# Expert outputs of a decoder layer: from one DRAM row per pick to two running sums per token

## The chip, the cores and the metric

The kernel runs on one core of a Trainium2 chip. The metric is device microseconds of one execution; lower is better. Times below are the median of several runs, and the profile is of one further execution.

## What is computed

One decoder layer over 8 sequences of 128 tokens with 256 features, so 1,024 tokens. Self-attention (sliding window) and cross-attention come first and are each added to the residual; the change touches only the feed-forward part that follows. That part is, cut to what matters:

```python
shared = silu_and_mul(x @ shared_gate_up_w.T) @ shared_down_w.T      # 704 hidden units
shared = shared * sigmoid(x @ sgate_w.T)
topk_w, topk_ids = top_k(softmax(x @ gate_w.T), 4)                   # 16 experts, 4 picks per token
for e in range(16):
    coef = sum(where(topk_ids == e, topk_w, 0), axis=-1)
    acc = acc + (silu_and_mul(x @ w13[e].T) @ w2[e].T) * coef[:, None]
out = x_residual + shared + acc
```

So every token receives the sum of four expert outputs, each 256 float32 numbers (1 KB).

## The kernel before

The program is written by hand for each engine: SP issues plain DMAs in the order written, GpSimd (POOL) issues indirect DMAs, and semaphores tie the engines together. A tile is the 128 tokens of one sequence; there are B = 8 tiles.

**Routing and blocks.** Once a tile's top four experts are known, GpSimd scatters each token row into `x_slots` in DRAM, sorted by expert (line 534, 32 indirect DMAs). The sorted rows are then worked off in NBLK = 47 blocks of 128 rows, each block of one expert; rows in a block that hold no token are padding.

**The block stage.** For block n, SP loads 128 token rows (`xb`, `load_rows`, line 426) and the expert's down weights (`w2`, `load_down`, line 433), in turn, one of each per block. TensorE (PE) turns the rows, computes gate and up, turns the hidden rows and computes the down product. VectorE (DVE) scales the result by the routing weight into one of RB = 4 buffers `yb` (`take_block`, line 1271). It also works out `ids`, the 128 DRAM rows to which the block's output goes (`block_ids`, line 1280). GpSimd's `place_rows` (line 607) then scatters the 128 rows of `yb` to `y_picks` in DRAM: one row per pick, 4,096 in all, and rows of their own behind them for padding. No row is written twice, and `place_rows` waits for nothing but its `yb` and its `ids`. `take_block` n waits until the scatter of block n - 4, which read the same buffer, has landed (`yb_placed`).

**The end.** TensorE still has the second half (tiles 4 to 7) of the shared expert to do: chunks 6 to 11, as `down(6)`, `rows_of(8)`, `down(7)`, `rows_of(9)`, and so on to `down(11)`. `rows_of(n)` computes gate and up products of chunk n, `down(n)` its down product; each `down(n)` needs `hid_h` and `hid_l` of its chunk, which ScalarE (ACT) and DVE make. Beside that, SP waits for the landing of all 47 scatters and loads `y_picks` back into `yg`, one DMA of 512 KB for each tile (line 451), four rows per token. DVE adds the four rows of a token and the residual in `combine`, three instructions per tile. These stand in DVE's queue between the chunk work in a fixed order: `gated(8)`, `low_hidden(8)`, two tiles of `combine`, `gated(9)`, `low_hidden(9)`, two tiles, `gated(10)`, `low_hidden(10)`, two tiles, `gated(11)`, `low_hidden(11)`, one tile, `finish(1)`, one tile, then the four additions of the shared result (line 1329). `gated` (line 1160) is the first DVE step of a chunk and `low_hidden` (line 1165) the last; between them ACT makes `hid_h` (line 743). `finish` (line 1171) copies half of the down result out, `turn_rows` (line 1651) turns it. Tiles 0 to 3 are stored after their `combine`, tiles 4 to 7 after the additions of line 1329.

`link(ins)` makes DVE wait for the instruction's own completion before its next one.

**Zeros.** While attention runs, SP also fills `x_slots` with zeros from the tile `zero_b` (line 412, 16 DMAs). `load_keys(7)` is the last DMA of that loop; after it SP waits for the shared weights and loads two small tables (lines 417, 418).

Of the kernel before, what the change touches and what calls it, by code (L numbers as in the profile page):

```python
# [7 lines left out]
F32 = mybir.dt.float32  # L8
# [5 lines left out]
ALU = mybir.AluOpType  # L14
# [3 lines left out]
B, T, D = 8, 128, 256  # L18
# [9 lines left out]
TOPK = 4  # L28
# [11 lines left out]
RB = 4  # L40
# [4 lines left out]
YROW = PICKS + NBLK * 128  # L45
# [13 lines left out]
def decoder_layer(nc, x_in, ctx_in, keys_in, wqkv_in, bqkv_in, wo_in, bo_in, rope_in, masks_in, gate_in,  # L59
                  w13_in, w2_in, shared_in, ident_in, iota_in, tri_in, upto_in, table_in, picks_in, dump_in, packs_in, out):  # L60
    ctx = ExitStack()
    with ctx:
# [6 lines left out]
        def sem(name):  # L69
            return ctx.enter_context(nc.semaphore(name))  # L70
# [5 lines left out]
        def place(name, shape, dt=F32):  # L76

            n = 1
            for extent in shape[1:]:
                n *= extent  # L80
            at = cursor[0]
            cursor[0] = at + -(-n * mybir.dt.size(dt) // 32) * 32
            return nc.alloc_sbuf_tensor_at(name, shape, dt, offset=at)
# [91 lines left out]
        yg = place("yg", [128, B, TOPK, D])  # L175
# [53 lines left out]
        y_picks = nc.dram_tensor("y_picks", [YROW, D], F32)  # L229
# [136 lines left out]
        gathered = [sem(f"gathered{b}") for b in range(B)]  # L366
# [12 lines left out]
        def _(sp):  # L379
# [35 lines left out]

            sp.wait_ge(swl_ready, SC)
# [33 lines left out]
            for b in range(B):  # L450
                sp.dma_start(yg[:, b, :, :], y_picks[T * TOPK * b:T * TOPK * (b + 1), :].rearrange("(p k) d -> p k d", k=TOPK)
                             ).then_inc(gathered[b], 16)

            for b in range(B):
                sp.wait_ge(x_out_ready, b + 1)
                sp.dma_start(out[b], x2[:, b, :]).then_inc(y_stored, 16)
            sp.wait_ge(y_stored, 16 * B)
# [3 lines left out]
        def _(pool):  # L461
# [141 lines left out]
            def place_rows(n):  # L603

                pool.wait_ge(yb_ready, n + 1)
                pool.wait_ge(ids_ready, n + 1)
                pool.indirect_dma_start(y_picks[:, :], bass.IndirectOffsetOnAxis(ids[:, n:n + 1], 0),  # L607
                                        yb[:, n % RB, :], None).then_inc(yb_placed[n % RB], 16)
# [230 lines left out]
        def _(dve):  # L839
# [5 lines left out]
            def link(ins):  # L845

                links[0] += 1
                ins.then_inc(chain1, 1)
                dve.wait_ge(chain1, links[0])
# [449 lines left out]
            def combine(first, last):  # L1299

                for b, step in (divmod(i, 3) for i in range(first, last)):
                    if step == 0:
                        dve.wait_ge(gathered[b], 16)
                        link(dve.tensor_tensor(yg[:, b, 0:2, :], yg[:, b, 0:2, :], yg[:, b, 2:4, :], ALU.add))  # L1304
                    elif step == 1:
                        link(dve.tensor_tensor(yg[:, b, 0, :], yg[:, b, 0, :], yg[:, b, 1, :], ALU.add))
                    else:
                        ins = dve.tensor_tensor(x2[:, b, :], yg[:, b, 0, :], x2[:, b, :], ALU.add)
                        if b < HB:
                            ins.then_inc(x_out_ready, 1)  # L1310
                        else:
                            link(ins)

            dve.wait_ge(rows_added, HB)
            done = 0
            for n, more in zip(range(SC + AHEAD, 2 * SC), (6, 6, 6, 0)):
                gated(n)
                low_hidden(n)
                combine(done, done + more)
                done += more  # L1320
            combine(done, done + 3)
            finish(1)
            combine(done + 3, 3 * B)
# [480 lines left out]
def lay_out(inputs):  # L1804
# [51 lines left out]
    pick = np.arange(PICKS, dtype=f).reshape(B, T, TOPK) - f(UNPLACED)  # L1856
    got["picks_in"] = pick.transpose(1, 0, 2)
    got["dump_in"] = (PICKS + np.arange(128)[:, None] + 128 * np.arange(NBLK)[None, :]).astype(f)
# [18 lines left out]
```

## Time and profile before

| what | value |
|---|---|
| median of 3 runs | 355.84 us |
| lowest and highest run | 354.18 and 358.53 us |
| profiled execution, its own time | 359.31 us |
| span of the profiled execution | 357.5 us |
| PE busy | 312.9 us (88% of the span) |
| DVE busy | 247.5 us (69%) |
| ACT busy | 186.6 us (52%) |
| POOL busy | 149.0 us (42%) |
| mean granted TensorE clock | 0.944 of full speed |

The span runs from the first to the last recorded work of the core, and 1.81 us of the execution's own time lie outside it. Attention and routing fill the first 206 us of the span. The block stage runs to about 327 us; the first scatter of block outputs starts at 218.2 us. The end takes the remaining 30 us. A row of the timeline gives the start and the duration in us, the engine, the line and the operation, and in brackets how long the engine sat idle before it and who released it. A count such as x2 or x8 means that many instructions merged in one row.

### The profile page before, as it was taken

The page shows a single profiled execution, that of the slowest core. Times are in us where ns is not written, and L with a number is a line of the kernel's source. Part 1 is how long each engine was busy: PE and PEld are TensorE (multiplying, and loading weights), DVE is VectorE, ACT ScalarE, POOL GpSimd, SP SyncE. Part 2 cuts the span into 40 slices and gives each one's busy share as a digit, 9 for nine tenths or more (in the row PEclk, how much of TensorE's full clock was granted, in tenths as well). Part 3 has the DMA queues.
Part 4 walks back from the last instruction along what each step waited for, and adds up shares of the span by engine and source line. Part 5 has one row for each costly group of instructions (what it writes and reads, how often), then busy time and mean ns, then how long its engine had stood idle before and what let it go on. Part 6 is the DMA issues. An engine that isn't in the chain of part 4 may idle for free.

```text
span 357.5 us, 8484 instructions
## 1 busy us (share of the span) xinstructions
PE 312.9 (88%) x2594; PEld 242.3 (68%) x2595; DVE 247.5 (69%) x733; ACT 186.6 (52%) x537; POOL 149.0 (42%) x179
## 2 busy tenths in 40 slices
PE   8857799999999997869989569998999999899953
PEld 3334576767667775647767459887888989798732
DVE  2353778888888769574878966666667767673785
ACT  1033689898898858467368314343444444332210
POOL 2580424435554304177876832344343444434000
PEclk9986999999999879996999959999999999999996
DMA  5996086989799831012232524777677777773931
GB/s 206 287 397 265 4 243 201 300 226 312 236 254 282 234 102 31 0 63 108 78 110 77 149 64 149 228 221 223 202 227 221 220 226 231 217 210 103 380 132 59
DMA packets 44185, 66.84 MB, mean 187 GB/s; under 512 B 5379, under 2 KB 32020, under 8 KB 43636
## 3 DMA queue, kind: packets, MB, share of 16 engines
q1 hardware_dynamic: 39508, 54.91, 51.0%
q0 software_dynamic: 3792, 10.56, 7.9%
q10 hardware_dynamic: 848, 0.92, 0.8%
q8 instruction: 19, 0.31, 0.4%
q14 instruction: 18, 0.15, 0.1%
HBM read 37.07 MB, written 29.30 MB: 186 GB/s over the span
## 4 chain that ended last, share of the span: by engine, by line
PE 35%; issue 23%; POOL 16%; DVE 13%; ACT 6%; DMA 4%; SPq 0%; POOLq 0%; DVEq 0%; ACTq 0%
POOL y_picks L607 12%; PE bank L1492 7%; PE bank L1418 6%; PE bank L1409 5%; PE bank L1362 4%; POOL x_slots L534 3%; PE bank L1427 3%; ACT probs L644 2%; PE bank L1451 2%; PE bank L1404 2%; PE bank L1530 2%; PE bank L1466 2%; DVE yg L1304 1%; DVE neg_max L895 1%; DMA yg<-y_picks 1%
## 5 line engine op out<-in xcount | busy, mean ns | idle before, releaser
L607 POOL DMA_INDIRECT y_picks<-yb,ids x47 | 45.1, 959 | 73.9 <-DVE yb L1271 73.3
L644 ACT ACTIVATE probs<-bank,neg_max 128x128 f32<-128x128 f32 x256 | 70.6, 401 | 2.8 <-DVE neg_max L895 2.8
L895 DVE TENSOR_REDUCE neg_max<-bank 128x4 f32<-128x512 f32 x64 | 42.1, 683 | 11.8 <-PE bank L1409 11.6
L1762 PE MATMUL bank<-w,hbt 128*128 128x256 f32 x188 | 48.2, 380 | 0.0
L1418 PE MATMUL bank<-ident,probs 128*128 128x128 f32 x256 | 39.8, 297 | 3.0 <-ACT probs L644 3.0
L534 POOL DMA_INDIRECT x_slots<-x,slots x32 | 36.7, 1147 | 10.8 <-issue 8.9
L1418 PEld LDWEIGHTS bank<-ident,probs 128*128 128x128 f32 x256 | 31.6, 152 | 11.6 <-ACT probs L644 7.8
L804 ACT ACTIVATE xbt_h<-bank 128x256 fp32r<-128x256 f32 x47 | 18.1, 384 | 40.1 <-PE bank L1732 40.0
L1762 PEld LDWEIGHTS bank<-w,hbt 128*128 128x128 f32 x188 | 32.1, 190 | 2.5
L1264 DVE TENSOR_TENSOR hb<-sg,bank 128x176 f32<-128x176 f32 x47 | 15.8, 337 | 24.4 <-ACT sg L812 24.4
L812 ACT ACTIVATE sg<-bank 128x176 f32<-128x176 f32 x47 | 14.9, 317 | 30.4 <-PE bank L1492 30.4
L1732 PE MATMUL bank<-ident,xb 128*128 128x128 f32 x94 | 19.1, 287 | 10.4 <-POOL w_l L600 7.4
L1492 PE MATMUL bank<-w_h,xbt_h 128*128 x94 | 27.6, 375 | 0.0
L1256 DVE TENSOR_TENSOR xbt_l<-bank,xbt_h 128x256 fp32r<-128x256 f32 x47 | 19.9, 424 | 9.7 <-ACT xbt_h L804 5.8
L1271 DVE TENSOR_SCALAR yb<-bank,offset 128x256 f32<-128x256 f32 x47 | 22.7, 483 | 2.6 <-PE bank L1762 2.6
L1732 PEld LDWEIGHTS bank<-ident,xb 128*128 128x128 f32 x94 | 12.8, 146 | 17.2 <-issue 7.6
L1492 PE MATMUL bank<-w_h,xbt_l 128*128 x94 | 23.4, 331 | 0.0
L1492 PE MATMUL bank<-w_l,xbt_h 128*128 x94 | 23.3, 330 | 0.0
L481 POOL TENSOR_TENSOR turned<-qkv,rope 128x320 f32<-128x320 f32 x8 | 6.9, 865 | 37.2 <-DVE qkv L876 37.2
L743 ACT ACTIVATE hid_h<-hid 128x512 fp32r<-128x512 f32 x12 | 7.6, 632 | 28.3 <-DVE hid L1160 28.3
L505 POOL TENSOR_TENSOR rstd<-ve,expo 128x1 f32<-128x1 f32 x16 | 9.4, 590 | 28.5 <-DVE ve L945 28.4
L1752 PE MATMUL bank<-ident,hb 128*128 128x128 f32 x94 | 18.2, 275 | 1.3 <-issue 1.2
(175 smaller groups left out, 694.9 us busy)
## 6 DMA issues: line engine op xcount, KB each, us to landing
x_slots<-zero_b SPq DMA_DIRECT2D x16, 1072.0 KB, 10.5
w<-w_in_dram SPq DMA_DIRECT2D x47, 256.0 KB, 3.1
xb<-x_slots SPq DMA_DIRECT2D x47, 134.0 KB, 2.8
w<-w_in_dram SPq DMA_DIRECT2D x4, 1408.0 KB, 12.9
yg<-y_picks SPq DMA_DIRECT2D x8, 512.0 KB, 7.1
sw_raw<-shared_in_dram SPq DMA_DIRECT2D x6, 384.0 KB, 3.3
ktc<-keys_in_dram SPq DMA_DIRECT2D x8, 256.0 KB, 3.0
ctx_sb<-ctx_in_dram SPq DMA_DIRECT2D x1, 1024.0 KB, 13.3
```

The source lines that it names most:

```text
L534: pool.indirect_dma_start(x_slots[:, :], bass.IndirectOffsetOnAxis(slots[:, TOPK * b + k:TOPK * b + k + 1], 0), x[:, b, :], None).then_inc ...
L607: pool.indirect_dma_start(y_picks[:, :], bass.IndirectOffsetOnAxis(ids[:, n:n + 1], 0), yb[:, n % RB, :], None).then_inc(yb_placed[n % RB] ...
L644: ins = act.activation(probs[:, g, j, :], ps_s[kind][g][:, 128 * j:128 * j + 128], ACT.Exp, bias=neg_max[:, kind, g, j:j + 1])
L804: act.activation(xbt_h[:, n % 2, :, :], ps_xt[n % 2][:, 0:KC * 128].rearrange("p (k n) -> p k n", k=KC), ACT.Copy).then_inc(xbt_high, 1)
L895: dve.tensor_reduce(neg_max[:, kind, g, :], ps_s[kind][g].rearrange("p (j n) -> p j n", j=BLK), AX.X, ALU.max, negate=True).then_inc(max_r ...
L1256: dve.tensor_tensor(xbt_l[:, n % 2, :, :], ps_xt[n % 2][:, 0:KC * 128].rearrange("p (k n) -> p k n", k=KC), xbt_h[:, n % 2, :, :].bitcast( ...
L1271: dve.tensor_scalar(yb[:, n % RB, :], ps_yb[n % 2][:, 0:D], offset[:, n % RB, 1:2], None, ALU.mult).then_inc(yb_ready, 1)
L1418: ins = pe.transpose(ps_s[kind][g][:, 128 * j:128 * j + 128], probs[:, g, j, :], ident[:, :])
L1492: ins = pe.matmul(outs, w, m, start=first and i == 0, stop=last and i == len(todo) - 1, skip_group_check=not (first and last))
L1732: ins = pe.transpose(ps_xt[n % 2][:, 128 * k:128 * k + 128], xb[:, n % RB, 128 * k:128 * k + 128], ident[:, :])
L1752: ins = pe.transpose(ps_ht[n % 2][:, 128 * k:128 * k + 128], hb[:, n % 2, 128 * k:128 * k + 128], ident[:, :])
L1762: ins = pe.matmul(ps_yb[n % 2][:, 0:D], hbt[:, n % 2, k, :], w2[:, n % RB, k, :], start=k == 0, stop=k == KC - 1)
```

## The change

Block outputs are no longer placed in a row of their own. GpSimd's scatter becomes an adding one: each block's 128 rows are added to rows of one of two arrays in DRAM, `y_sum0` and `y_sum1`, which have one row per token. Even blocks go to the first, odd blocks to the second. A token's four experts fall into different blocks, and two additions to one row may not overlap, so scatter n now waits until scatter n - 2 has landed. The two arrays are filled with zeros by two DMAs of 1 MB during attention, and the first two scatters wait for them. At the end two rows per token are loaded, in four DMAs (two halves by two sums) of 512 KB each, and `combine` handles two tiles in two instructions: sum plus sum, then plus residual. `combine(3)`, the last, now stands ahead of `finish(1)`. Tiles 0 to 3 are stored in two DMAs in place of four. The tables of row numbers hold the token's row in place of the pick's. The diff, without the declarations of semaphores and without the index tables:

```diff
-YROW = PICKS + NBLK * 128
+YROW = B * T + NBLK * 128
+SUMS = 2
...
-        yg = place("yg", [128, B, TOPK, D])
+        yg = place("yg", [128, SUMS, B, D])
...
-        y_picks = nc.dram_tensor("y_picks", [YROW, D], F32)
+        y_sums = [nc.dram_tensor(f"y_sum{i}", [YROW, D], F32) for i in range(SUMS)]
...
+            for i in range(SUMS):
+                sp.dma_start(y_sums[i][0:B * T, :].rearrange("(p r) d -> p r d", p=128),
+                             zero_b[:, 0:2 * D].bitcast(F32).unsqueeze(1).broadcast_to([128, B, D])).then_inc(sums_zeroed, 16)
+
             sp.wait_ge(swl_ready, SC)
             sp.dma_start(ends[:, :, :, :], table_in).then_inc(table_loaded, 16)
...
             for r in range(RB):
                 sp.wait_ge(yb_placed[r], 16 * len(range(r, NBLK, RB)))
-            for b in range(B):
-                sp.dma_start(yg[:, b, :, :], y_picks[T * TOPK * b:T * TOPK * (b + 1), :].rearrange("(p k) d -> p k d", k=TOPK)
-                             ).then_inc(gathered[b], 16)
-
-            for b in range(B):
-                sp.wait_ge(x_out_ready, b + 1)
+            for half in range(NHALF):
+                for i in range(SUMS):
+                    sp.dma_start(yg[:, i, HB * half:HB * half + HB, :],
+                                 y_sums[i][0:B * T, :].rearrange("(p b) d -> p b d", b=B)[:, HB * half:HB * half + HB, :]
+                                 ).then_inc(gathered[half], 16)
+
+            for pair in range(HB // 2):
+                sp.wait_ge(x_out_ready, pair + 1)
+                sp.dma_start(out[2 * pair:2 * pair + 2].rearrange("b p d -> p b d"), x2[:, 2 * pair:2 * pair + 2, :]
+                             ).then_inc(y_stored, 16)
+            for b in range(HB, B):
+                sp.wait_ge(x_out_ready, HB // 2 + b - HB + 1)
                 sp.dma_start(out[b], x2[:, b, :]).then_inc(y_stored, 16)
...
                 pool.wait_ge(yb_ready, n + 1)
                 pool.wait_ge(ids_ready, n + 1)
-                pool.indirect_dma_start(y_picks[:, :], bass.IndirectOffsetOnAxis(ids[:, n:n + 1], 0),
-                                        yb[:, n % RB, :], None).then_inc(yb_placed[n % RB], 16)
+                if n < SUMS:
+                    pool.wait_ge(sums_zeroed, 16 * SUMS)
+                else:
+
+                    pool.wait_ge(yb_placed[(n - SUMS) % RB], 16 * ((n - SUMS) // RB + 1))
+                pool.indirect_dma_start(y_sums[n % SUMS][:, :], bass.IndirectOffsetOnAxis(ids[:, n:n + 1], 0),
+                                        yb[:, n % RB, :], None, compute_op=ALU.add).then_inc(yb_placed[n % RB], 16)
...
-            def combine(first, last):
-
-                for b, step in (divmod(i, 3) for i in range(first, last)):
-                    if step == 0:
-                        dve.wait_ge(gathered[b], 16)
-                        link(dve.tensor_tensor(yg[:, b, 0:2, :], yg[:, b, 0:2, :], yg[:, b, 2:4, :], ALU.add))
-                    elif step == 1:
-                        link(dve.tensor_tensor(yg[:, b, 0, :], yg[:, b, 0, :], yg[:, b, 1, :], ALU.add))
-                    else:
-                        ins = dve.tensor_tensor(x2[:, b, :], yg[:, b, 0, :], x2[:, b, :], ALU.add)
-                        if b < HB:
-                            ins.then_inc(x_out_ready, 1)
-                        else:
-                            link(ins)
+            def combine(pair):
+
+                bs = slice(2 * pair, 2 * pair + 2)
+                dve.wait_ge(gathered[pair // 2], 16 * SUMS)
+                link(dve.tensor_tensor(yg[:, 0, bs, :], yg[:, 0, bs, :], yg[:, 1, bs, :], ALU.add))
+                ins = dve.tensor_tensor(x2[:, bs, :], yg[:, 0, bs, :], x2[:, bs, :], ALU.add)
+                if pair < HB // 2:
+                    ins.then_inc(x_out_ready, 1)
+                else:
+                    link(ins)
 
             dve.wait_ge(rows_added, HB)
-            done = 0
-            for n, more in zip(range(SC + AHEAD, 2 * SC), (6, 6, 6, 0)):
+            for n in range(SC + AHEAD, 2 * SC):
                 gated(n)
                 low_hidden(n)
-                combine(done, done + more)
-                done += more
-            combine(done, done + 3)
+                combine(n - SC - AHEAD)
             finish(1)
-            combine(done + 3, 3 * B)
```

## Rows read from the trace of the kernel before

**Rows 1.** Busy time in stretches of the block stage and the end.
```profile
core 0: us, PE busy (x) PEld busy (x) DVE busy (x) ACT busy (x) POOL busy (x), PEclk, DMA share, GB/s
265.00:312.00 47.00, 45.35 (x278) 40.78 (x276) 32.50 (x120) 19.53 (x59) 18.90 (x21) 1.00 0.75 225
327.00:357.50 30.50, 20.71 (x84) 15.31 (x83) 19.47 (x37) 5.29 (x9) 0.50 (x1) 0.90 0.47 178
```

**Rows 2.** GpSimd's timeline: the first and the last scatters of block outputs, 47 in all.
```profile
218.20 0.98 POOL L607 DMA_INDIRECT y_picks<-yb,ids  x1 [9.72 <-DVE yb L1271]
...
319.69 0.96 POOL L607 DMA_INDIRECT y_picks<-yb,ids  x1 [1.31 <-DVE yb L1271]
321.95 0.96 POOL L607 DMA_INDIRECT y_picks<-yb,ids  x1 [1.30 <-DVE yb L1271]
324.01 0.96 POOL L607 DMA_INDIRECT y_picks<-yb,ids  x1 [1.10 <-DVE yb L1271]
...
326.54 0.96 POOL L607 DMA_INDIRECT y_picks<-yb,ids  x1 [0.30 <-issue]
```

**Rows 3.** Chain that ended last, at the turn from scatter to load.
```profile
323.80 0.22 issue
...
326.54 2.39 DMA y_picks<-yb,ids
329.08 3.53 DMA yg<-y_picks
```

**Rows 4.** Tile yg from 329.5 us on, without the first load.
```profile
L451 SPq DMA_DIRECT2D yg<-y_picks x7: 426/433/451, 329.5 to 332.3; - x7
...
DMA to landing us min/median/max: 4.4/7.5/9.8
```

**Rows 5.** Tile xb, loads of 128 rows from DRAM: landing.
```profile
DMA to landing us min/median/max: 2.1/2.8/4.0
```

**Rows 6.** DMA queues from 218 to 327 us (packets, MB, share of 16 engines).
```profile
q1 hardware_dynamic: 12347, 17.26, 57.4%
q0 software_dynamic: 2181, 5.99, 14.3%
```

**Rows 7.** Timeline of the end: DVE, and PE's last transposes.
```profile
332.64 0.69 DVE L1304 TENSOR_TENSOR yg<-yg 128x512 f32<-128x512 f32 x1 [1.08 <-DMA yg<-y_picks]
...
335.68 0.68 DVE L1160 TENSOR_TENSOR hid<-silu,bank 128x512 f32<-128x512 f32 x1
337.06 0.69 DVE L1165 TENSOR_TENSOR hid_l<-hid,hid_h 128x512 fp32r<-128x512 f32 x1 [0.70 <-ACT hid_h L743]
...
340.71 0.68 DVE L1160 TENSOR_TENSOR hid<-silu,bank 128x512 f32<-128x512 f32 x1
...
345.98 0.69 DVE L1160 TENSOR_TENSOR hid<-silu,bank 128x512 f32<-128x512 f32 x1
...
351.98 1.06 PE L1651 MATMUL bank<-ident,y_t 128*128 128x128 f32 x8 [0.95 <-DVE y_t L1171]
...
353.39 1.66 DVE L1329 SCALAR_TENSOR_TENSOR x<-bank,sig,x 128x256 f32<-128x256 f32 x4
```

**Rows 8.** Busy time of PE in stretches of the end (columns as in rows 1).
```profile
337.60:342.50 4.90, 4.46 (x19) 3.30 (x18) 4.06 (x9) 1.07 (x2) 0.00 (x0) 1.00 1.02 393
342.50:348.10 5.60, 1.67 (x6) 1.05 (x6) 4.70 (x10) 0.67 (x2) 0.00 (x0) 0.99 0.04 12
348.10:351.10 3.00, 2.92 (x6) 1.82 (x6) 1.41 (x3) 0.03 (x1) 0.00 (x0) 0.50 0.00 0
```

**Rows 9.** SP's timeline, from the keys' last load to the weights' first.
```profile
139.01 0.33 SPq L397 DMA_DIRECT2D ktc<-keys_in_dram  x1
...
196.04 2.62 SPq L433 DMA_DIRECT2D w<-w_in_dram  x3
```

**Rows 10.** DMA issues: the zeros of x_slots (count, KB each, us to landing).
```profile
x_slots<-zero_b SPq DMA_DIRECT2D x16, 1072.0 KB, 10.5
```

**Rows 11.** SP's longest waits in the block stage (us in total, times, longest).
```profile
SPq L432 <- PE bank L1762: 1.9, 5, 0.8
SPq L424 <- DVE ids L1280: 1.8, 3, 1.0
```

More of the change, by code:

```diff
@@ L365, in decoder_layer @@
         yb_ready = sem("yb_ready")
-        gathered = [sem(f"gathered{b}") for b in range(B)]
+        sums_zeroed = sem("sums_zeroed")
+        gathered = [sem(f"gathered{half}") for half in range(NHALF)]
         x_out_ready = sem("x_out_ready")
@@ L449, in _ @@
                 sp.wait_ge(yb_placed[r], 16 * len(range(r, NBLK, RB)))
-            for b in range(B):
-                sp.dma_start(yg[:, b, :, :], y_picks[T * TOPK * b:T * TOPK * (b + 1), :].rearrange("(p k) d -> p k d", k=TOPK)
-                             ).then_inc(gathered[b], 16)
-            for b in range(B):
-                sp.wait_ge(x_out_ready, b + 1)
+            for half in range(NHALF):
[9 more added lines that the diff above has]
+                sp.wait_ge(x_out_ready, HB // 2 + b - HB + 1)
                 sp.dma_start(out[b], x2[:, b, :]).then_inc(y_stored, 16)
-            sp.wait_ge(y_stored, 16 * B)
+            sp.wait_ge(y_stored, 16 * (HB // 2 + HB))
         @block.gpsimd
@@ L1855, in lay_out @@
     got["table_in"] = np.stack([np.stack([0 * n, 128 * n]), np.stack([0 * n + NE - 1, 0 * n + EMPTY])])[None].astype(f)
-    pick = np.arange(PICKS, dtype=f).reshape(B, T, TOPK) - f(UNPLACED)
-    got["picks_in"] = pick.transpose(1, 0, 2)
-    got["dump_in"] = (PICKS + np.arange(128)[:, None] + 128 * np.arange(NBLK)[None, :]).astype(f)
+    row = np.arange(B * T, dtype=f).reshape(T, B, 1) - f(UNPLACED)
+    got["picks_in"] = np.tile(row, (1, 1, TOPK))
+    got["dump_in"] = (B * T + np.arange(128)[:, None] + 128 * np.arange(NBLK)[None, :]).astype(f)
     got["packs_in"] = (float(NE) ** (np.arange(WORDS * PACK) % PACK)).astype(f)[None, :]
```

## The prediction

> **What bounds the kernel now.** I read the busy time by stretches first. In the block stage PE is busy 45.35 of 47 us at full clock and the DMA engines 0.75 of the time; in the last 30.5 us PE is busy 20.71 us only, at 0.90 of the clock [rows 1]. So the blocks are paced by PE together with what SP feeds it (SP's two longest kinds of wait come to 3.7 us in 8 waits over that stage [rows 11], so it hardly ever had time over), and GpSimd is not the bound: each scatter occupies it 0.96 us and it then sits idle 1.3 us until the next `yb` [rows 2]. The chain of waits is the second view; it names the scatter all through the stage, but each of those links begins at a `yb`, so it follows the blocks' own pace. Its end is real, though: last scatter, 2.39 us to its landing, gather, DVE [rows 3].
>
> The end is the third view. DVE's timeline sets it. From 332.64 us on DVE pauses only the 0.7 us in which ACT makes each `hid_h`: `combine` of two tiles stands before each `gated`, so `gated` starts at 335.68, 340.71 and 345.98, some 5 us apart [rows 7], while PE's work per chunk fits in 4.46 of 4.9 us [rows 8]. PE finds its last hidden chunk late: between 342.5 and 348.1 us it works 1.67 of 5.6 us, and then does the same six matmuls of `down(11)` in 2.92 us at 0.50 of the clock, so 1.25 us more [rows 8].
>
> **The change part by part.**
>
> *Zeros.* Two more 1 MB DMAs at about 139.4 us on SP. Behind them stand two loads of small tables, then the weight loads of 196 us [rows 9]; two issues and two landings of 10.5 us each [rows 10] end by about 161 us even back to back. Cost nothing; the cover is the 35 us from then to 196, in which SP has nothing else to issue. Without it, it would cost the 21 us.
>
> *The wait in the scatter.* Let L be the time from a scatter's start on GpSimd to its landing. The plain one takes 2.39 us in a quiet moment [rows 3]. Behind the waiting scatter only later scatters are queued; who waits for them is DVE's `take_block` four blocks on, through it PE, and at the end SP's gather. A scatter may start 0.2 us after the landing of the one two before it (GpSimd's wake of 0.22 us [rows 3]). From the 1st scatter (218.20) to the 45th (324.01) are 22 steps of two, 4.81 us each [rows 2]; so the wait costs the stage nothing while L + 0.2 stays under 4.81, L under 4.61. Above it GpSimd's two chains pace the stage, and each 0.1 us of L costs 2.3 us.
>
> *What L becomes.* The trace holds no adding DMA. Lower bound: the destination is read while the source is, nothing added, 2.39. Upper bound: the read of 128 rows goes first and costs as much as a load of 128 rows from DRAM does in this stage, 2.8 us median [rows 5]: 5.2. That load's time includes an issue and a completion which the scatter already pays, so I take the part in between, 1.2 us: L = 3.6 in quiet. Among other traffic the same load goes from 2.1 (least) to 2.8 us [rows 5]; with 0.7 more, L is 4.3 in the stage, 0.3 under the limit. I therefore cost the stage at nothing, with little to spare.
>
> The scatters hold the DMA engines 14.3% of the stage and SP's loads 57.4% [rows 6]; a second read of the same rows makes some 86 to 89% with the rest: still not full. The Trainium skill, Collectives: The Full Stack, section The bandwidth ceiling: the fold count and why AG ≠ RS ≠ AR, says that an add in the DMA path costs no compute time but two source reads, so twice the read traffic. By it the packets of one scatter (14.3% of 109 us over 47, 0.33 us) would double, L would be 2.7 and the sum 5.1 us of gain; no row here shows an adding DMA, and my sum doesn't use it.
>
> *The start of the gather.* The last blocks come faster than 2.27 us, so here the wait does bite. The 47th scatter waits for the 45th: 324.01 + 3.6 + 0.2 = 327.8 in place of 326.54; it lands at 331.4 and the gather is issued at 331.55 (329.08 before [rows 3]). In general the gather starts at 324.36 + 2L.
>
> *The gather.* Half as many bytes, but the first `combine` now needs two DMAs. Before, the first landed 3.53 us after issue [rows 3], the second at 329.5 + 4.4 = 333.9, which is 4.8 us after the first issue [rows 4]. So `combine(0)` starts at 331.55 + 4.8 = 336.4, against 332.64: DVE stands 3.7 us longer ahead of it, and behind it in the queue waits `gated(9)`.
>
> *The additions.* Six instructions for two tiles took 3.04 us net (332.64 to 335.68 [rows 7]). Now two of 128x512, of the form of line 1304 at 0.69 us [rows 7]: 1.4 us, saving 1.6 us a pair. DVE then runs: `combine(0)` 336.4, `gated(9)` 337.8 (335.68 before); `gated` to the end of `low_hidden` is 2.07 us (335.68 to 337.75 [rows 7]), so 339.9; `combine(1)` to 341.3, `gated(10)` to 343.35, `combine(2)` (both linked, 1.44) to 344.8, `gated(11)`, and `low_hidden(11)` is done at 346.85 (345.98 + 2.07, 348.05, before). PE between: `down(9)` at 339.95, `rows_of(11)` until about 344.4, just ahead of `gated(11)`; the other gathered half is long there (two more DMAs, last of four).
>
> *After that.* PE idles about 1 us ahead of `down(11)`, where it had 3.9. After 3.9 us the clock had halved, with 0.44 us idle in 337.6 to 342.5 it stood at 1.00 [rows 8]; 1 us is nearer the latter, so I take 1.67 us for the six matmuls: PE ends at 348.55, against 351.05. If the clock still falls, 2.92 us, 1.25 later. `combine(3)` now runs beside `down(11)` and is hidden by it; before, the last tile's three additions held the last four back until 353.39, while the first half of the eight transposes that they need was done at 352.5 [rows 7]: with 0.05 us for the signal, 0.84 us saved. The rest, PE's end to the span's end, was 6.45 us and becomes 5.6. The span ends at 348.55 + 5.6 = 354.15.
>
> *Sum.* 357.5 - 354.15 = 3.35 us less. In general, 10.55 - 2L. The profiled execution took 359.31 us, 3.47 above the median of the runs; I take the difference against the median: 355.84 - 3.35 = 352.5 us.
>
> **The rivals.**
>
> *A: the add is nearly free* (L 2.4 to 3.0). The gain is 10.55 - 2L, 5.8 to 4.5 us: 350.0 to 351.3. For it: the scatter's packets are only 0.33 us of engine time. Against: the destination has to come from DRAM first.
>
> *B: the wait becomes the pace* (slower). From L = 4.61 on the 47th scatter starts at 218.2 + 23(L + 0.2), lands L later, and from there the end needs 0.15 + 4.8 + 17.75 us (336.4 to 354.15 above). L = 4.8 gives a span of 360.7 (359.0 us against the median); 4.95 gives 364.3 (362.6); 5.2 gives 370.1 (368.4 us). It decides at L = 4.66, where gain and loss cancel. For it: the upper bound, and loads that take up to 4.0 us in this stage, 1.9 over the least [rows 5]. Against: four of them would have to be slow in a row, since `yb` has four buffers. The Trainium skill, DMA: Bandwidth & Descriptors, section Latency and other measured facts, gives DRAM access as 0.2 us on average and 2 us at high load. Were each scatter to pay that 2 us with the doubled packets, L would be 2.39 + 0.33 + 2.0 = 4.7, just at the turning point; the spread of 1.9 us in the loads agrees with it, the median of 0.7 over the least does not.
>
> *C: the clock or the gather eats the gain.* If the 2 us that PE then idles ahead of `down(9)` drop the clock, `rows_of(11)` and both `down` lose some 1.3 to 4 us (2.92 for 1.67 on each `down` [rows 8]): 353.8 to 356.5. The same time comes with L of 4.3 to 4.6 also in the last scatters.
>
> *D: the DMA engines fill.* If an added row costs three times its packets, they stand at 0.75 + 0.29, 1.04 of the stage [rows 1, 6]: 4% of 109 us is 4.4 us lost against 3.35 gained: about 357.
>
> **How the numbers follow.** My case, L of 3.0 to 4.3: 0.38, 351 to 354. A 0.14. C 0.17. D 0.05. B 0.26; of it 0.21 beyond L = 4.95. A measurement of this kernel tells about 2% (7.1 us) from no change: the runs shown lie 4.3 us apart. Faster by that needs 348.7 us or less, beyond even the free add (350.0), so it can come only from A with something more: 0.08. Slower by that needs 363.0, L near 5: 0.21 of B and 0.02 of D, so 0.23. The rest, 0.69, is within 2%. The range of 8 in 10 goes from 349.5, just past the free add, to 368.4, the upper bound of L; for my case and A and C alone it would be 349.5 to 356.5.
>
> **What would show it.** GpSimd's idle time ahead of line 607's scatters should still end at DVE's `yb` for nearly all 47, and scatters 2.27 us apart. If it ends at a DMA landing on `y_sums`, with the spacing above 2.4 us, B holds. `combine(0)` should wait for the gather until about 336 us, `gated(9)`, `gated(10)`, `gated(11)` should stand 3.5 us apart, and `down(11)` should run its six matmuls in 1.67 us. The forecast is wrong if the scatter's start-to-landing time exceeds 4.6 us in the stage, if GpSimd itself needs over 2.3 us to issue an adding scatter, or if SP's loads land late enough to stop PE in every block.

## The result and the profile after

The changed kernel takes 373.76 us in the median of 4 runs, against 357.18 us for the kernel before (4 runs). The ratio is 1.044, with a 95% interval from 1.032 to 1.057: slower, where the forecast was 3.35 us faster. It is above the top of the range (368.4 us) as well. The ratios here and below leave out runs in a slower state of the chip (379.19 us at a granted clock of 0.93 is one), so they are not quite the quotients of the medians. The profiled execution took 370.99 us with a span of 369.2 us.

Two stretches tell most of it. From the first to the last scatter of block outputs it was 108.3 us before (218.20 to 326.54, [rows 2]) and is 123.8 us now. From the last scatter to the end of the span it was 31.0 us and is 30.8 us. So the block stage lost 15.5 us, and the end, which was to bring 3.35, brought 0.2. The scatters also began 3.6 us earlier in this execution than in the profiled one of before (214.64 against 218.20). That part of the program is not touched except for the zeros, and other profiles below start at 215 to 222 us, so nothing is read into it.

GpSimd's timeline, some of the 47 scatters (start, duration, what; in brackets the idle time before it and who ended it):

```profile
214.64 1.63 POOL L624 DMA_INDIRECT y_sum<-yb,ids  x1 [9.49 <-DVE yb L1288]
216.90 1.57 POOL L624 DMA_INDIRECT y_sum<-yb,ids  x1 [0.64 <-DVE yb L1288]
220.11 1.55 POOL L624 DMA_INDIRECT y_sum<-yb,ids  x1 [1.64 <-DMA y_sum<-yb,ids]
...
336.09 1.54 POOL L624 DMA_INDIRECT y_sum<-yb,ids  x1 [0.67 <-issue]
338.42 1.55 POOL L624 DMA_INDIRECT y_sum<-yb,ids  x1 [0.78 <-DMA y_sum<-yb,ids]
```

A scatter occupies GpSimd for 1.55 us where it was 0.96 [rows 2], and the third one already waits for the landing of the first. From the 1st to the 47th are 23 steps of two, 5.38 us each, where two blocks took 4.81 before. The chain that ended last, from 324 us on (start, duration, what), shows what one such step is made of:

```profile
324.77 3.94 DMA y_sum<-yb,ids
328.70 0.03 issue
328.73 0.02 DVEq L1287
328.75 0.05 issue
328.80 0.50 DVE yb L1288
329.30 0.16 issue
329.46 3.65 DMA y_sum<-yb,ids
...
333.86 3.80 DMA y_sum<-yb,ids
337.67 0.02 issue
337.69 0.04 POOLq L623
337.73 0.47 issue
338.20 0.22 POOLq L63
338.42 3.58 DMA y_sum<-yb,ids
342.00 0.02 issue
```

The last scatter, with little traffic beside it, lands after 3.58 us. The scatter begun at 324.77 lands at 328.70, and the next one into the same sum starts at 329.46, 0.76 us later. The chain puts a `yb` in between; that `yb` was released by the same landing but belongs to a later block, so it is not what the scatter waited for. The last step shows it without one (POOLq is GpSimd's queue, L623 the new wait). DVE's row for the 47th and last `yb`:

```profile
333.20 0.48 DVE L1288 TENSOR_SCALAR yb<-bank,offset 128x256 f32<-128x256 f32 x1 [2.05 <-DMA y_sum<-yb,ids]
```

It was ready at 333.68. The 45th scatter landed at 337.67 and the 47th started at 338.42, 0.75 us later. DVE, released by the landing at 328.70, started 0.10 us after it (328.80), so the delay is GpSimd's own; it is called its wake here. Paired in order, each scatter from the fifth on starts 1.2 to 6.6 us after its own `yb` was ready. So a row of this kernel that names a `yb` as what ended GpSimd's idle time often names the wrong one: what ended it was a landing.

The next rows are for the tile `y_sum` (scatters only, block stage) and for the DMA queues from 210 to 340 us:

```profile
DMA to landing us min/median/max: 3.6/4.7/6.0
...
q1 hardware_dynamic: 12528, 17.44, 48.2%
q0 software_dynamic: 6624, 6.03, 35.1%
```

One adding scatter counts about 6,624 / 47 = 141 packets, a plain one about 2,181 / 47 = 46 [rows 6]: three times as many. (Both windows cut off the end of the last scatters.) The scatters hold the DMA engines for 35.1% of 130 us, 45.6 us, where it was 14.3% of 109 us, 15.6 us: 2.9 times as long. The two shares are only 2.5 apart because the stage has become longer. The stage in two halves and the end, with columns as in [rows 1]:

```profile
214.00:262.00 48.00, 44.58 (x265) 38.99 (x263) 31.52 (x115) 19.03 (x57) 27.17 (x18) 1.00 0.90 205
262.00:310.00 48.00, 44.22 (x263) 39.19 (x264) 27.98 (x107) 18.34 (x56) 27.09 (x18) 1.00 0.92 202
...
340.00:369.00 29.00, 13.98 (x52) 10.28 (x50) 11.57 (x19) 3.57 (x6) 0.00 (x0) 0.81 0.37 113
```

The engines are now 90 to 92% busy, where [rows 1] has 0.75. The waits of that stage (us in total, times, longest) and the landing of `xb`:

```profile
POOL y_sum L624 <- DVE yb L1288: 35.9, 25, 9.5
...
DVE yb L1288 <- DMA y_sum<-yb,ids: 22.1, 19, 2.0
POOL y_sum L624 <- DMA y_sum<-yb,ids: 20.5, 14, 2.3
PEld bank L1741 <- DMA xb<-x_slots: 11.8, 11, 2.3
...
DMA to landing us min/median/max: 2.0/3.3/5.1
```

So there are two suspects. GpSimd and DVE wait for scatters to land, which no engine did before; GpSimd's 20.5 us are too few, since most of the 25 waits put down to a `yb` are landings too. And the token rows `xb` take longer (5.1 us at most, 4.0 before [rows 5]), so TensorE's weight loads wait 11.8 us for them. DVE at the end, then TensorE's first matmul after its wait, then the six matmuls that begin with it (columns as in [rows 1]):

```profile
334.88 0.69 DVE L1177 TENSOR_TENSOR hid<-silu,bank 128x512 f32<-128x512 f32 x1 [1.20 <-PE bank L1501]
...
349.18 0.69 DVE L1320 TENSOR_TENSOR yg<-yg 128x512 f32<-128x512 f32 x1 [12.21 <-DMA yg<-y_sum]
...
350.51 0.68 DVE L1177 TENSOR_TENSOR hid<-silu,bank 128x512 f32<-128x512 f32 x1
...
353.83 0.68 DVE L1177 TENSOR_TENSOR hid<-silu,bank 128x512 f32<-128x512 f32 x1
...
352.64 0.80 PE L1501 MATMUL bank<-hid_h,sw_h 128*128 128x512 f32 x1 [9.60 <-DVE hid_l L1182]
...
352.64:355.36 2.72, 2.72 (x6) 2.17 (x7) 1.99 (x4) 0.63 (x1) 0.00 (x0) 0.50 0.18 63
```

The additions are as quick as forecast: `gated(10)` follows `gated(9)` after 3.3 us, where it was 5.0 [rows 7]. But the first addition stands 12.2 us waiting for the gather, and `gated(9)` (350.51) waits behind it. TensorE idles 9.6 us and then does the six matmuls of `down(9)` at half clock, in 2.7 us; over the end stretch its granted clock is 0.81.

### The profile page after: what moved, and what is told of

It reads as the page before. It is cut to its first block and busy times, and to the rows that moved or that the text cites. A ratio compares the mean times of both kernels' runs of the same rounds, so it can differ in the third digit from the quotient of the medians.

```text
span 369.2 us, 8463 instructions
## 1 busy us (share of the span) xinstructions
PE 313.2 (85%) x2595; PEld 241.2 (65%) x2595; DVE 239.2 (65%) x717; ACT 186.5 (51%) x537; POOL 176.8 (48%) x179
## 5 line engine op out<-in xcount | busy, mean ns | idle before, releaser
L624 POOL DMA_INDIRECT y_sum<-yb,ids x47 | 72.9, 1550 | 62.0 <-DVE yb L1288 35.9
L821 ACT ACTIVATE xbt_h<-bank 128x256 fp32r<-128x256 f32 x47 | 18.0, 384 | 45.6 <-PE bank L1741 44.8
L1427 PE MATMUL bank<-ident,probs 128*128 128x128 f32 x256 | 38.6, 290 | 3.0 <-ACT probs L661 3.0
L1427 PEld LDWEIGHTS bank<-ident,probs 128*128 128x128 f32 x256 | 30.6, 148 | 10.8 <-ACT probs L661 8.6
L1741 PEld LDWEIGHTS bank<-ident,xb 128*128 128x128 f32 x94 | 12.5, 145 | 22.9 <-DMA xb<-x_slots 11.8
L1501 PE MATMUL bank<-hid_h,sw_h 128*128 128x512 f32 x24 | 10.6, 442 | 11.3 <-DVE hid_l L1182 11.3
```

Source lines behind the costliest of these rows:

```text
L624: pool.indirect_dma_start(y_sums[n % SUMS][:, :], bass.IndirectOffsetOnAxis(ids[:, n:n + 1], 0), yb[:, n % RB, :], None, compute_op=ALU.ad ...
L821: act.activation(xbt_h[:, n % 2, :, :], ps_xt[n % 2][:, 0:KC * 128].rearrange("p (k n) -> p k n", k=KC), ACT.Copy).then_inc(xbt_high, 1)
L1427: ins = pe.transpose(ps_s[kind][g][:, 128 * j:128 * j + 128], probs[:, g, j, :], ident[:, :])
L1501: ins = pe.matmul(outs, w, m, start=first and i == 0, stop=last and i == len(todo) - 1, skip_group_check=not (first and last))
L1741: ins = pe.transpose(ps_xt[n % 2][:, 128 * k:128 * k + 128], xb[:, n % RB, 128 * k:128 * k + 128], ident[:, :])
```

## The experiments

Theory W: the new wait paces the stage, landing plus GpSimd's wake, over two blocks. Theory T, its rival: what costs is the DMA time of an adding scatter, which makes SP's loads late, wait or no wait. The table gives, for each profiled execution, the time from the first to the last scatter, from there to the end of the span, and the median of the timed runs with its ratio to the kernel before on the same chip (one run for one sum).

| kernel | first to last scatter | last scatter to end | us | ratio, interval |
|---|---|---|---|---|
| before | 108.3 | 31.0 | 357.18 | |
| changed | 123.8 | 30.8 | 373.76 | 1.044 (1.032 to 1.057) |
| four sums | 115.7 | 36.1 | 370.72 | 1.033 (1.021 to 1.044) |
| plain scatters with the wait | 109.8 | 28.7 | 355.26 | 0.984 (0.974 to 0.995) |
| new end alone | 108.8 | 25.4 | 354.82 | 0.983 (0.969 to 0.996) |
| chunks first | 127.8 | 22.5 | 368.53 | 1.023 (1.014 to 1.032) |
| one sum | 218.6 | 26.0 | 465.14 | |
| half weights | 118.1 | 30.7 | 366.29 | 1.022 (1.011 to 1.032) |
| four sums, half weights | 109.6 | 35.8 | 369.58 | 1.037 (1.029 to 1.046) |
| three sums, chunks first | 116.2 | 31.1 | 364.95 | 1.019 (1.007 to 1.031) |
| GpSimd adds | 107.8 | 31.0 | 358.44 | 1.003 (0.999 to 1.008) |

The block stage of "chunks first" is the same code as the changed kernel's. Its 127.8 against 123.8 us shows how far two profiles of a stage that waits lie apart. Stages in which scatters hardly ever wait repeat more closely: 107.8 to 108.8 us in the three with plain scatters and no wait, 115.7 and 116.2 us with four and three sums.

**Four sums** take the wait away, not the adds:

```diff
-SUMS = 2
+SUMS = 4
...
+                link(dve.tensor_tensor(yg[:, 0:2, bs, :].rearrange("p s b d -> p s (b d)"),
+                                       yg[:, 0:2, bs, :].rearrange("p s b d -> p s (b d)"),
+                                       yg[:, 2:4, bs, :].rearrange("p s b d -> p s (b d)"), ALU.add))
                 link(dve.tensor_tensor(yg[:, 0, bs, :], yg[:, 0, bs, :], yg[:, 1, bs, :], ALU.add))
```

> The changed kernel with four sums in place of two, so that a scatter's wait for the one four before it is already met by the four yb buffers; adds, their packets and their 1.55 us on GpSimd stay. Zeros and the gather double, each pair of tiles takes one more DVE addition. Theory W (the wait for the scatter two before paces the stage, landing about 4.65 us plus 0.75 until GpSimd starts, 5.38 for two blocks): first to last scatter falls from 123.8 to 108 to 111 us, total 356 to 361 us. Theory T (the adding scatters' DMA time, 35% of the engines against 14%, delays SP's loads and so TensorE): first to last scatter stays at 118 to 124 us, total 367 to 375 us.

Measured: 115.7 us from first to last scatter, between the two theories, and 370.72 us in total, in theory T's range, though the longer end has a part in that. GpSimd no longer waits for any landing. Its waits, the DMA queues from 216 to 322 us, and the idle time ahead of TensorE's reads of `xb` in this kernel:

```profile
POOL y_sum L624 <- DVE yb L1288: 54.2, 46, 10.1
...
q1 hardware_dynamic: 11871, 16.50, 54.0%
q0 software_dynamic: 5896, 5.37, 41.8%
...
  DMA xb<-x_slots: 19.5, 29
```

The wait alone accounts for 8.1 of the 15.5 us (123.8 - 115.7), or up to 12 by the second look at the stage (127.8). 7.4 us remain although nothing waits for a scatter, with the DMA engines 96% busy and 19.5 us in 29 waits of TensorE's weight loads and matmuls for `xb` (9.0 us in 14 before). The end grew: with four rows per token the first addition waits 9.7 us for four DMAs, and DVE's next chunk behind it.

**Plain scatters with the wait** take the add away, not the wait:

```diff
-                                        yb[:, n % RB, :], None, compute_op=ALU.add).then_inc(yb_placed[n % RB], 16)
+                                        yb[:, n % RB, :], None).then_inc(yb_placed[n % RB], 16)
```

> The changed kernel with its wait, but with plain scatters: rows overwrite each other instead of adding up, so three of four expert outputs of most tokens are left out. Theory W, with a plain landing of 2.4 to 3.1 us plus 0.75, below the 4.6 us of two blocks: first to last scatter about 108 us, total 351 to 355 us. Were the wait itself dear on GpSimd whatever the DMA does, the stage would stay at 120 us or more and the total near 370 us. Theory T gives 108 us too, since the packets are plain.

Measured: 109.8 us for the stage and a total 1.6% under the kernel before: the wait by itself is nearly free. (The profiled execution took 358.39 us, 3.1 above the median of its runs, so its stage is if anything too long.) It also lets one read how long a plain scatter takes among the stage's traffic, which no row of before showed. Tile `y_sum`, scatters of the stage alone, and GpSimd's waits for landings:

```profile
DMA to landing us min/median/max: 2.4/3.4/4.5
...
POOL y_sum L624 <- DMA y_sum<-yb,ids: 11.6, 6, 2.6
```

3.4 us in the median, 1.0 above the quiet 2.4. With 0.75 us of wake that is 4.15 us, under the 4.5 of two blocks at their usual 2.27 us, and only six of the waits are put down to a landing.

**The new end alone** has plain scatters without waits into a row per pick, and loads two of the four rows:

```diff
-                                 y_sums[i][0:B * T, :].rearrange("(p b) d -> p b d", b=B)[:, HB * half:HB * half + HB, :]
+                                 y_picks[B * T * i:B * T * (i + 1), :].rearrange("(p b) d -> p b d", b=B)[:, HB * half:HB * half + HB, :]
...
-                pool.indirect_dma_start(y_sums[n % SUMS][:, :], bass.IndirectOffsetOnAxis(ids[:, n:n + 1], 0),
-                                        yb[:, n % RB, :], None, compute_op=ALU.add).then_inc(yb_placed[n % RB], 16)
+                pool.indirect_dma_start(y_picks[:, :], bass.IndirectOffsetOnAxis(ids[:, n:n + 1], 0),
+                                        yb[:, n % RB, :], None).then_inc(yb_placed[n % RB], 16)
```

> The end of the change alone: plain scatters to a row per pick without waits, then two of the four rows per token loaded and added two tiles at a time (the other two rows are left out of the sum). By the forecast's steps the end is worth 10.55 - 2L with L = 2.39, 5.8 us: total 350 us. Rival: the first addition waits longer, because both halves of a pair have to land (6.6 us from issue instead of 3.5), DVE's next chunk waits behind it and the gain is 0 to 3 us: 353 to 357 us.

Measured: from the last scatter to the end 25.4 us, 5.6 under before (31.0), where 5.8 was worked out. The timed runs give 4.2 us between the medians (358.98 to 354.82), and the interval reaches from 0.969 to 0.996, so the two expectations are parted by the profile rather than by the clock. DVE and TensorE at that end, the second row with columns as in [rows 1]:

```profile
334.29 0.69 DVE L1310 TENSOR_TENSOR yg<-yg 128x512 f32<-128x512 f32 x1 [2.77 <-DMA yg<-y_picks]
...
344.00:346.20 2.20, 1.67 (x6) 1.05 (x6) 1.74 (x3) 0.00 (x0) 0.00 (x0) 1.00 0.00 0
```

The last six matmuls run in 1.67 us at full clock, as forecast. So the working of the end was right for a gather that starts with the blocks' end.

**Chunks first** gives `gated` the way free in the changed kernel:

```diff
                 low_hidden(n)
-                combine(n - SC - AHEAD)
             finish(1)
+            for pair in range(B // 2):
+                combine(pair)
```

> The changed kernel with DVE's additions moved behind its chunk work, so that no gated waits behind a gather. If the end is held by that order (DVE stands 12.2 us ahead of the first addition while TensorE idles 9.6 us and then runs at half clock): TensorE is done at about 347 us of the span, the additions end at about 355, the span at about 359, total 359 to 363 us, some 10 us below the changed kernel. If the gather's landing alone sets the end, the gain is under 3 us. The block stage stays at about 124 us under either.

Measured: 22.5 us from the last scatter to the end, 8.3 less than the changed kernel, and 1.023 in place of 1.044 of the time before. The gather still begins late (349.91 us), but `gated(11)` waits for TensorE and not for it:

```profile
354.25 0.69 DVE L1177 TENSOR_TENSOR hid<-silu,bank 128x512 f32<-128x512 f32 x1 [2.10 <-PE bank L1502]
```

So about 8 us at the changed kernel's end are DVE's fixed order, met by a late gather. The total of 368.53 us lies above the 359 to 363 that were expected: TensorE was done at 358 us of the span and not at 347. The first scatter came 3.5 us later than in the changed kernel's profile and the stage took 4.0 us more, which is 7.5 of the 11 us; the rest was not traced.

**One sum** makes every scatter wait for the one before (`SUMS = 1`, and one addition less in `combine`).

> The changed kernel with one sum in place of two, so every adding scatter waits for the one before it; half the zeros, half the gather, one DVE addition less per pair. Theory W (landing plus 0.75 us paces the stage): the blocks come every 4.35 us (landing 3.6, as in quiet) to 5.5 us (4.75, as among other traffic), first to last scatter 200 to 253 us against 123.8, total 440 to 500 us. If the stage is set by the DMA engines' time alone it stays near 124 us and the total under 375 us.

Measured: 218.6 us for 46 steps, 4.75 us a block, and 465.14 us. The scatter's landing falls to 3.8 us in the median, as less traffic runs beside it (the engines are 58% busy from 220 to 320 us), and 3.8 plus 0.75 is 4.55. Tile `y_sum`, scatters only, what GpSimd's idle time before them is put down to, and their landing:

```profile
  DVE yb L1288: 148.1, 44
...
DMA to landing us min/median/max: 3.6/3.8/5.5
```

Each of these scatters has to wait for the landing of the one before, and still the view names a `yb` for 44 of them: the same wrong name as above.

**Half weights** lighten the traffic and keep the wait:

```diff
+                ks = KC if n < RB else 1
-                sp.dma_start(w2[:, n % RB, :, :].rearrange("p k d -> p (k d)"),
-                             w2_in[bass.ds(e, 1)].rearrange("e p k d -> p (e k d)")).then_inc(w2_loaded[n % RB], 16)
+                sp.dma_start(w2[:, n % RB, 0:ks, :].rearrange("p k d -> p (k d)"),
+                             w2_in[bass.ds(e, 1), :, 0:ks, :].rearrange("e p k d -> p (e k d)")).then_inc(w2_loaded[n % RB], 16)
```

> The changed kernel (two sums, wait kept) with only the first half of each block's down weights loaded from the fifth block on; the other half is left over from an earlier block, so half of each down product uses wrong weights, the work is the same. SP's traffic in the block stage falls by about a third. If the landing of an adding scatter is long because of the traffic beside it, it falls from 4.7 to about 4.2 us and first to last scatter to 112 to 116 us, total 359 to 364 us. If the landing is the add's own, the stage stays above 120 us and the total above 367 us.

Measured: the landing falls from 4.7 to 4.3 us, the stage from 123.8 to 118.1 and the total to 366.29 us, 1.022 of before. The direction is the one expected of a landing that is long because of the traffic; stage and total came out 2 us above the ranges given. (4.3 + 0.75) x 23 is 116 us.

**Four sums, half weights** ask whether the rest that four sums left is DMA time; the edits are those of the two runs together.

> Four sums (no wait on an earlier scatter beyond the one for the yb buffer) and half of the down weights loaded from the fifth block on (the rest as in the half-weights run). With four sums alone first to last scatter took 115.7 us, 7.4 more than before the change. If that rest is DMA time (engines 96% busy there, rows of xb landing late), it goes: 107 to 110 us, and TensorE's waits for xb fall under 8 us. If it comes from GpSimd's longer issue (1.55 us against 0.96) or from anything else that adds do, it stays at 113 us or more.

Measured: 109.6 us, 6.1 of the 7.4 us gone, with GpSimd's 1.55 us and all adds in place. The idle time ahead of TensorE's reads of `xb`, and the busy time of a stretch (columns as in [rows 1]):

```profile
  DMA xb<-x_slots: 9.4, 16
...
222.00:270.00 48.00, 46.07 (x274) 40.34 (x273) 31.65 (x118) 19.62 (x59) 30.81 (x20) 1.00 0.84 166
270.00:318.00 48.00, 46.48 (x284) 41.79 (x282) 32.76 (x122) 19.91 (x60) 30.93 (x20) 1.00 0.89 169
```

`xb` is late 9.4 us, as before the change (9.0 in 14 waits there), and the DMA engines are at 0.84 to 0.89. So most of the rest was DMA time (theory T). The kernel before was not run with half weights; that lighter loads alone would not have quickened its stage is argued, from TensorE's busy share, 0.96 to 0.97 of the stretch in both. The waits for `xb` did not fall under 8 us as expected, but to the old level.

GpSimd's longer issue costs nothing in the middle of the stage, but it does at its end. The last three scatters of this run:

```profile
327.67 1.56 POOL L625 DMA_INDIRECT y_sum<-yb,ids  x1 [0.32 <-DVE yb L1289]
329.53 1.55 POOL L625 DMA_INDIRECT y_sum<-yb,ids  x1 [0.30 <-DVE yb L1289]
331.38 1.55 POOL L625 DMA_INDIRECT y_sum<-yb,ids  x1 [0.30 <-issue]
```

They stand 1.86 us apart, back to back on GpSimd; before, the last three took 2.53 us for the two steps (324.01 to 326.54 [rows 2]) and here 3.71. That is 1.2 of the 1.3 us still left.

**Three sums, chunks first** puts both repairs together (`SUMS = 3`, one addition more per pair, and the order of "chunks first").

> Both repairs on the changed kernel: three sums (a scatter waits for the one three before it) and DVE's additions behind its chunk work. If wait, traffic and DVE's order add up as the single runs say: landing 5.1 plus 0.75 over three blocks is 1.95 us, under the block's own 2.3, so only the traffic is left in the stage: first to last scatter 114 to 117 us, then 24 to 27 us to the end, total 356 to 361 us, level with the kernel before. If the traffic alone sets the stage whatever the waits, as in the second look at two sums (127.8 us), it stays above 120 us and the total above 364 us.

Measured: 116.2 us for the stage, as expected. But the end took 31.1 us, not 24 to 27, and the total is 364.95 us, 1.9% over before. With the scatters no longer lagging, TensorE's end at 349.9 us is what the additions wait for, and all twelve of them (350.49 to 358.95) stand exposed behind it.

**GpSimd adds** is the kernel before with another end:

```diff
+            for b in range(B):
+                pool.wait_ge(gathered[b], 16)
+                pool.tensor_tensor(yg[:, b, 0:2, :], yg[:, b, 0:2, :], yg[:, b, 2:4, :], ALU.add).then_inc(halved, 1)
...
+            gated(SC + 2)
+            low_hidden(SC + 2)
+            for n in range(SC + 3, 2 * SC):
+                gated(n)
+                low_hidden(n)
+                combine(2 * (n - SC - 3))
+                combine(2 * (n - SC - 3) + 1)
```

> The kernel before the change, with another end: plain scatters, four rows per token gathered as before, but GpSimd, idle by then, makes the first of the three additions of each tile (about 1.4 us for 512 columns by its 0.87 us for 320), and DVE's chunk work stands ahead of its additions. If the end was held by DVE's order, TensorE runs through, is done at about 346 us of the span, and the total is 350 to 352 us, 1 to 2% under the kernel before. If GpSimd slows DVE beside it or the gather sets the end, 354 to 358 us.

Measured: 358.44 us against 358.45, no difference. GpSimd's additions, and DVE's timeline with and without them beside it:

```profile
333.10 8.39 POOL L615 TENSOR_TENSOR yg<-yg 128x512 f32<-128x512 f32 x6 [0.24 <-DMA yg<-y_picks]
...
333.32 1.51 DVE L1306 TENSOR_TENSOR yg<-yg 128x256 f32<-128x256 f32 x1
...
341.96 0.41 DVE L1306 TENSOR_TENSOR yg<-yg 128x256 f32<-128x256 f32 x1
```

The same addition takes 1.51 us while GpSimd adds and 0.41 us afterwards. What DVE was spared it lost again to such slow additions. No version tried here beats the kernel before and computes the whole layer.

## Why the prediction was wrong

**The stage "at nothing".** This is the step that failed: the wait in the scatter was costed at nothing, and the stage lost 15.5 us. Its limit was L + 0.2 under 4.81, so L under 4.61, with L put at 4.3. Two of its three terms were off.

- *The wake.* 0.2 us was read from GpSimd's start after a DVE result [rows 3]. After a landing it is 0.75 us (337.67 to 338.42, and the same in the steps before). The limit on L was therefore about 4.06.
- *The traffic's share of L.* The 0.7 us was read from the loads of `xb` [rows 5]. A plain scatter goes from 2.4 in quiet to 3.4 in the stage (plain scatters with the wait; 3.5 with the new end alone), 1.0. The adding one goes from 3.6 to 4.7, 1.1.
- *What the add itself costs* was right: 1.2 us was taken, and it is 3.58 against 2.39 in quiet and 4.7 against 3.4 to 3.5 in the stage.

So L is 4.7 rather than 4.3, over a limit of 4.06 rather than 4.61.

**Rival B happened**, and its formula gives the stage once the wake is right: 23 steps of L + wake, 23 x (4.7 + 0.75), are 125 us, and 123.8 were measured. It had 0.26. One sum shows the same from the other side: 4.75 us for every block. (In B's own list the span for L = 5.2 comes to 370.3, not 370.1, which changes nothing.) The prediction's signs agree: L is over 4.6 us in the stage, and the spacing is 2.69 us, over 2.4. Only the sign of what ends GpSimd's idle time misleads, for the reason given above.

**Rival D happened too**, at 0.05 the least likely. It said that an added row might cost three times its packets, and that the engines would then stand at 1.04 of the stage; an adding scatter counts three times the packets and holds the engines 2.9 times as long. The prediction's own sum allowed the scatters a second 14.3% of the stage and called the engines not full. The 45.6 us that were measured are 42% of the old 109 us: 0.28 more, where 0.14 was allowed, and with 0.72 to 0.75 of before that is 1.00 to 1.03 of the old stage. So the old stage had no room to spare for them even without the wait.

The rule cited from the Trainium skill (Collectives: The Full Stack, section The bandwidth ceiling: the fold count and why AG ≠ RS ≠ AR), twice the read traffic and no compute time, was taken as double the packets. The runs here show three times the packets and 2.9 times the engines' time, so the measurement decides.

I had B and D as two ways to go. They add. Of the 15.5 us, 8.1 go when the wait goes (four sums), 6.1 more when the traffic beside the adds goes (four sums, half weights), and 1.2 of the last 1.3 are GpSimd's longer issue at the stage's end. They also feed each other, since the traffic lengthens L, so the split holds for the order in which these runs take things away, and a stage that waits differs by 4 us from one profile to the next.

L came out at 4.7, as 1.2 for the add and 1.1 for the traffic, and with the wake of 0.75 us that is beyond the turning point. The price of the other rule cited (the Trainium skill, DMA: Bandwidth & Descriptors, section Latency and other measured facts), 2 us for DRAM access at high load, had also given L = 4.7, at the turning point by a wake of 0.2 us; no run here shows the DRAM access by itself.

**The end** was right in its parts and wrong in what it hangs on. The additions and `down(11)` at full clock came as worked out, and the stretch behind TensorE's end took 5.7 us where 5.6 was worked out and 6.45 was before, with 5.6 us of gain where the gather starts with the blocks' end (new end alone). But the sum let the gather slip by 2.5 us only. Once scatters lag behind TensorE, which ran ahead through its chunks as far as `yb` let it, the gather slips by 13 us (342.15 against 329.08), and `gated(9)` waits behind it. The forecast named that queueing, and priced it for the small slip alone. The two DMAs of a half also take 7.0 us from the first issue (342.15 to 349.15) where 4.8 was taken from the loads of before [rows 4]. It is 7.0 us with plain scatters and the wait too (330.4 to 337.41), so the adds are not the reason. In the run with the new end alone, reading a single DRAM tensor, it was 5.2 us (329.05 to 334.29). Why two tensors read more slowly than one wasn't tried.

**What held:** the zeros cost nothing visible, GpSimd is not the bound at 1.55 us a scatter until the last three, and DVE's additions were halved.

The range's top was the upper bound of L in the formula of B, where each 0.1 us is 2.3 us. With a wake that no row of before shows for a landing, and the engine time of the packets as a third unknown, it should have reached beyond it.

## What to carry to other kernels

Before a wait on a DMA's completion is put into a pipeline, add the landing among the real traffic, the add's own extra and the engine's wake after a landing, and compare with the time that the pipeline gives. Here 4.7 + 0.75 stood against 4.5 to 4.81, while the quiet value, 3.6, seemed to fit. An adding scatter saves bytes at the end but pays in the stage that issues it: look at its packets, not its bytes, and compare the engines' time in us, not as shares of stages that differ in length. When a trace names a producer as what ended an idle time, check that it is the one of this very step. And where an in-order engine's queue mixes work that feeds another engine with work that waits for a late DMA, put the feeding work first, or else the lateness holds up the fed engine as well.

## What the runs showed of the hardware

- An adding indirect scatter of 128 rows of 1 KB counts three times the packets (about 141 against 46), holds the DMA engines 2.9 times as long (45.6 us against 15.6 for the stage), occupies GpSimd 1.55 us against 0.96, and lands after 3.6 us in quiet against 2.4 and after 4.7 in the stage against 3.4 to 3.5. The bytes that the profile counts for it are those of the plain one (6.03 MB against 5.99 MB for 47), so if the destination is read as well, it doesn't show there.
- A GpSimd scatter that waited for a landing started 0.75 us after it; after a DVE result it was 0.2 to 0.3 us. DVE started 0.10 us after the same kind of landing.
- A DVE addition with both operands in SBUF takes 1.51 us beside GpSimd additions and 0.41 without. The Trainium skill (SBUF — State Buffer, section Who interferes with whom) says that a DVE instruction with two SBUF inputs contends with a GpSimd instruction that reads SBUF; the trace agrees.
- After 9.6 us without work the granted TensorE clock was at half: the six matmuls of a `down`, 1.67 us at full clock, took 2.7 us (352.64 to 355.36, granted clock 0.50).
